# A two-layer attention block on one core: the opening's conditioning products, first transfers and first parts are laid out differently

## What is computed

```python
# layer 0
xn = x * rsqrt(mean(x*x) + 1e-6) * rms_w
scale, shift = split(cond @ w_cond)              # 512 x 512 weights
q, k, v = split((xn * (1 + scale) + shift) @ w_qkv)
q, k = rope(q), rope(k)
x = softmax(q k^T / 4) v @ w_out + x
# layer 1
xn = layer_norm(x, norm_w, norm_b)
q, k, v = xn @ q_w + q_b, xn @ k_w + k_b, (xn @ v_w + v_b) * mask
y = softmax(q k^T - 1e6 * (1 - mask)) v
scale, shift = split(silu(cond) @ emb_w + emb_b) # 512 x 512 weights
x = x + silu(layer_norm(y) * (1 + scale) + shift) @ out_w + out_b
```

## Time and profile before

| | |
|---|---|
| median of 3 runs | 514.0 us |
| the profiled execution | 513.65 us |
| its span, first to last instruction | 511.9 us |
| PE busy | 501.6 us (98%) |
| DVE, ACT, POOL busy | 80%, 68%, 43% |
| first row score starts | 40.31 us |
| mean granted clock of PE | 0.997 |

### The profile page before, as it was taken

One profiled execution on the slowest core, in us unless ns is written; L12 is line 12 of the kernel. 1 busy time (PEld: TensorE's weight loads), 2 busy tenths in 40 slices (PEclk: granted clock), 3 DMA queues, 4 the chain that ended last, 5 costly groups with the idle time before them and its releaser, 6 DMA issues.

```text
span 511.9 us, 9839 instructions
## 1 busy us (share of the span) xinstructions
PE 501.6 (98%) x3339; PEld 193.7 (38%) x3339; DVE 408.6 (80%) x1051; ACT 345.7 (68%) x679; POOL 219.9 (43%) x254
## 2 busy tenths in 40 slices
PE   9999899999999999999999999999999999999997
PEld 5553423333443244333443334332433333333234
DVE  4876897998897688966898678967899999999324
ACT  1552467776767675776768676777778778787863
POOL 3039749999143420832227430544573035005401
PEclk9999999999999999999999999999999999999999
DMA  6983232242214133110331123210431112211011
GB/s 243 351 273 101 75 103 75 66 143 82 77 53 125 41 125 121 46 43 8 119 125 44 42 90 114 68 33 32 125 124 44 43 43 85 81 46 44 2 41 42
DMA packets 43034, 45.26 MB, mean 88 GB/s; under 512 B 4436, under 2 KB 41572, under 8 KB 42600
## 3 DMA queue, kind: packets, MB, share of 16 engines
q1 hardware_dynamic: 42696, 42.79, 26.8%
q10 hardware_dynamic: 288, 1.84, 0.9%
HBM read 25.46 MB, written 18.87 MB: 87 GB/s over the span
## 4 chain that ended last, share of the span: by engine, by line
PE 74%; DVE 13%; issue 3%; ACT 2%; POOL 2%; DVEq 0%; ACTq 0%; POOLq 0%
PE bank L547 19%; PE bank L530 11%; PE bank L521 10%; PE bank L593 9%; PE bank L510 9%; DVE masked L870 8%; PE bank L621 5%; PE bank L604 5%; PE bank L562 2%; PE bank L582 2%; DVE row_max L873 1%; ACT probs L721 1%; PE bank L555 1%; PE bank L629 1%; POOL XN L844 1%
## 5 line engine op out<-in xcount | busy, mean ns | idle before, releaser
L721 ACT ACTIVATE probs<-bank 128x512 f32<-128x512 f32 x512 | 272.4, 601 | 82.0 <-PE bank L521 81.3
L873 DVE TENSOR_REDUCE row_max<-bank 128x1 f32<-128x512 f32 x256 | 163.0, 684 | 29.5 <-PE bank L530 27.8
L530 PE MATMUL bank<-k_s,q_s 64*128 64x512 f16 x512 | 183.0, 382 | 1.8 <-DVE row_max L873 1.2
L870 DVE CUSTOM_DVE_ANT_0 masked<-bank,mask_bias 128x512 bf16<-128x512 f32 x256 | 163.0, 687 | 13.0 <-PE bank L530 12.0
L510 PE MATMUL bank<-q_s,k_s 64*128 64x512 f16 x512 | 151.9, 381 | 0.9 <-ACT v_aug L789 0.5
L521 PE MATMUL bank<-shift,kx 64*128 64x512 f16 x512 | 148.8, 377 | 0.0
L547 PE MATMUL bank<-probs,v_aug 128*17 128x512 f32 x1024 | 135.4, 598 | 0.7 <-ACT probs L721 0.7
L530 PEld LDWEIGHTS bank<-k_s,q_s 64*128 64x128 f16 x512 | 46.3, 93 | 151.7 <-DVE row_max L870 67.1
L593 PE MATMUL bank<-xT,wqkv 128*128 128x512 f32 x128 | 61.8, 613 | 0.4 <-ACT xT L752 0.3
L521 PEld LDWEIGHTS bank<-shift,kx 64*128 64x128 f16 x512 | 46.9, 95 | 31.9
L510 PEld LDWEIGHTS bank<-q_s,k_s 64*128 64x128 f16 x512 | 31.7, 94 | 13.4 <-ACT probs L721 8.0
(11 more groups left out here) (112 smaller groups left out, 505.1 us busy)
## 6 DMA issues: line engine op xcount, KB each, us to landing
q_parts<-parts SPq DMA_DIRECT2D x64, 128.0 KB
k_parts<-parts SPq DMA_DIRECT2D x64, 128.0 KB
q_s<-q_parts SPq DMA_DIRECT2D x32, 256.0 KB, 2.8
k_s<-k_parts SPq DMA_DIRECT2D x32, 256.0 KB, 3.0
X<-in_x SPq DMA_DIRECT2D x4, 512.0 KB, 7.3
y<-X SPq DMA_DIRECT2D x7, 256.0 KB, 2.2
wc<-in_w_cond ACTq DMA_DIRECT2D x1, 1024.0 KB, 4.9
tables<-in_tables SPq DMA_DIRECT2D x4, 256.0 KB, 6.8
```

Source lines behind the costliest of these rows:

```text
L530: nc.tensor.matmul(bank, m.q_s[slot][rows, i, queries], m.k_s[slot][rows, i, :], start=True, stop=True).then_inc(q.d_made, 1)
L721: act.activation(m.probs[k][:, h, :], bank, ACT.Exp, scale=1.0 if s >= B * NG else float(DH) ** -0.5)\
L870: dve.tensor_tensor_reduce(m.masked[D["max", n, k, h] % ND][:, :], bank, m.mask_bias[:, b, :], 1.0, LOWEST, ALU.add, ALU.max, to)\
L873: dve.tensor_reduce(to, bank, AX.X, ALU.max).then_inc(q.d_done, 1)
```

## The change

- cond @ w_cond in two steps. Step 0: cond is stationary, padded to 32 columns, and w_cond moves, 4 matmuls of 512 columns, each block of 128 conditions in its own 32 output rows; ACT copies the 128x512 result to SBUF. Step 1: 4 matmuls with that copy as stationary operand and a matrix of zeros and ones, chosen, as moving one, which sum the four blocks and turn them round. silu(cond) @ emb_w is made in the same way, in two pieces instead of four.
- The first half of w_cond is loaded on ACT's queue, the second on SP's behind batch 0. The bulk is loaded in group 0 and emb_w behind the operands of group 2.
- POOL fills kx and makes chosen; DVE keeps kx0.
- DVE writes the second half of batch 0's xT, ACT the first.
- ACT normalises batch 2 behind ("qk", 0, 1, 3); POOL only batch 3, now behind the rotation of chunk 0 of batch 1.
- POOL issues the eight stores of the high parts and the two of chunk 2's low part; SP issues the six other low parts'. The high part of chunk 1 is made one step earlier in ACT's order.
- FIRST_BUSY goes from 14 to 17, the busy matmuls of the opening from 6, 6 and 3 to 4 and 2.

The diff, cut to its core (left out are names of semaphores and buffers, and waits that follow from the above; await_parts is what every wait for stored parts calls):

```diff
@@ -91,10 +91,11 @@
 PIECES = {
     0: ((), qk(0, 3, 1), (), ()),
     1: (qk(0, 3, 2), (), qk(0, 3, 3), ()),
-    2: ((("embed", 0),), (), (("embed", 1),), ()),
-    3: ((("embed", 2),), (), (("embed", 3),), ()),
+    2: ((), (), (), (("embed", 1),)),
     4: (v(0, 3)[:1], (), (), ()),
 }
+
+BESIDE_VALUES = {(1, 2): ("embed", 0)}
 for _b in range(B):
     _s = 5 + NG * _b
@@ -127,15 +128,16 @@
-FIRST_BUSY = 14
+FIRST_BUSY = 17
 LAST_BUSY = (10, 4)
 PIECES = spread(PIECES)
 OPENING = (
-    some(("modulate",)) + (("busy", 6),) + some(*turn("p0", 0)) + (("busy", 6),) + some(*qk(0, 0, 0, 1, 2, 3))
-    + some(*v(0, 0)[:1], *turn("p0", 1), *v(0, 0)[1:], *qk(0, 1, 0, 1, 2, 3), *v(0, 1), *turn("p0", 2)) + (("busy", 3),)
+    some(("modulate", 0)) + (("busy", 4),) + some(("modulate", 1), *turn("p0", 0)) + (("busy", 2),)
+    + some(*qk(0, 0, 0, 1, 2, 3))
+    + some(*v(0, 0)[:1], *turn("p0", 1), *v(0, 0)[1:], *qk(0, 1, 0, 1, 2, 3), *v(0, 1), *turn("p0", 2))
     + maxima(0, 0, 1, 0, 3) + some(*qk(0, 2, 0))
     + maxima(0, 0, 2) + maxima(0, 1, 1, 0) + some(*qk(0, 2, 1))
     + maxima(0, 1, 3, 2) + maxima(0, 2, 1) + some(*qk(0, 2, 2))
@@ -164,7 +166,7 @@
     PARTS_AT[8 + NG * _b] = ((B + _b, 0), (B + _b, 1))
     PARTS_AT[9 + NG * _b] = ((B + _b, 2), (B + _b, 3))
-HIGH_BEHIND = [("qk", 0, 0, 2), ("turn", "p0", 1, 0), ("turn", "p0", 1, 1), ("v", 0, 0, 1)]
+HIGH_BEHIND = [("qk", 0, 0, 2), ("qk", 0, 0, 3), ("turn", "p0", 1, 1), ("v", 0, 0, 1)]
 OUT_AT = {25: 0, 29: 1, 32: 2}
@@ -199,6 +201,8 @@
             yield op, s - 1
         if op == "maxima" and k == TURNED and exists(s + 1):
             yield op, s + 1
+        if op == "maxima" and (s, k) in BESIDE_VALUES:
+            yield "piece", BESIDE_VALUES[s, k]
         if op == "values" and (s or k):
             yield (op, s, k - 1) if k else (op, s - 1, KT - 1)
@@ -208,6 +212,12 @@
     for s in range(GROUPS):
         for k in range(KT):
             yield from key_tile(s, k)
+
+
+def for_dve(piece):
...
@@ -622,13 +655,24 @@
                                         start=(k == 0), stop=(k == CT - 1))
         last.then_inc(q.d_made, 1)
-    def conditioning(piece, vector, chunks):
-        bank = d_free(D[piece])
-        for c in chunks:
+    def conditioning(piece, vector):
+
+
+        kind, step = piece
+        if step == 0:
+            bank = a_free(A[piece])
             for k in range(KC):
-                last = nc.tensor.matmul(bank[:, c * B:(c + 1) * B], m.wc[:, k, c * P:(c + 1) * P], vector[:, k, :],
-                                        start=(k == 0), stop=(k == KC - 1))
-        last.then_inc(q.d_made, 1)
+                last = nc.tensor.matmul(bank[W32 * k:W32 * (k + 1), :], vector[:, k, :], m.wc[:, k, :],
+                                        start=True, stop=True, tile_position=(0, W32 * k), skip_group_check=True)
+            last.then_inc(q.a_made, 1)
+        else:
+            bank = d_free(D[piece])
+            pe.wait_ge(q.chosen_step, B)
+            pe.wait_ge(q.a_done, A[kind, 0] + 1)
+            for c in range(KC):
+                last = nc.tensor.matmul(bank[:, c * B:(c + 1) * B], m.conditions[:, c * P:(c + 1) * P], m.chosen[:, :],
+                                        start=True, stop=True)
+            last.then_inc(q.d_made, 1)
     def keep_busy(count, bank):
...
@@ -805,7 +858,20 @@
                 act.activation(last_tokens(m)[:, h, columns(p)], m.a_banks[CT * p + h][:, 0:2 * P], ACT.Silu,
                                bias=m.last_mod[:, 1, h, :], scale=m.last_mod[:, 0, h, :]).then_inc(q.last_silu, 1)
-    act.dma_start(m.wc[:, :, :], m.in_wc).then_inc(q.wc_in, 16)
+    def normal(b):
+        act.wait_ge(q.rstd0_made, b + 1)
+        if b == 2:
+            await_turned(act, q, ("p0", 0))
+        for t in range(TPB * b, TPB * b + TPB):
+            act.activation(m.XN[b % 2][:, t % TPB, :], m.X[:, t, :], ACT.Copy, scale=m.rstd["p0"][:, t:t + 1])\
+               .then_inc(q.xn_made, 1)
+
+    def high_part(i):
+
+        act.wait_ge(q.rope_dve, 3 * i + 3)
+        act.activation(m.parts[:, 0, i, :], m.roped[0][i % 2][:, :], ACT.Copy).then_inc(q.high_made, 1)
+
+    act.dma_start(m.wc[:, 0:KC // 2, :], m.in_wc[:, 0:KC // 2, :]).then_inc(q.wc_in, 16)
     act.wait_ge(q.cond_in, 16)
     act.activation(m.es[:, :, :], m.condT[:, :, :], ACT.Tanh, scale=0.5).then_inc(q.es_step, 1)
     act.wait_ge(q.x_in[0], 16)
@@ -822,20 +888,19 @@
         if op == "piece":
             piece, = at
             if piece == ("qk", 0, 0, 2):
-                act.wait_ge(q.rstd0_made, 2)
-                for t in range(TPB):
-                    act.activation(m.XN[1][:, t, :], m.X[:, TPB + t, :], ACT.Copy,
-                                   scale=m.rstd["p0"][:, TPB + t:TPB + t + 1]).then_inc(q.xn_made, 1)
+                normal(1)
             if piece[0] == "turn":
                 tokens(piece)
             if piece[0] == "qk":
                 queries_keys(piece)
             if piece[0] == "v":
                 token_values(piece)
+            if piece in (("modulate", 0), ("embed", 0)):
+                conditions(piece)
+            if piece == ("qk", 0, 1, 3):
+                normal(2)
             if piece in HIGH_BEHIND:
-                i = HIGH_BEHIND.index(piece)
-                act.wait_ge(q.rope_dve, 3 * i + 3)
-                act.activation(m.parts[:, 0, i, :], m.roped[0][i % 2][:, :], ACT.Copy).then_inc(q.high_made, 1)
+                high_part(HIGH_BEHIND.index(piece))
     last_batch()
...
@@ -931,18 +996,16 @@
     def opening():
         dve.memset(m.idle[:, :], 0.0).then_inc(q.idle_made, 1)
         dve.memset(m.ACC, 0.0).then_inc(q.acc_zero, 1)
-        for t in (m.kx0[:, :], m.kx[:, :, :]):
-            dve.memset(t, 0.0).then_inc(q.units_made, 1)
+        dve.memset(m.kx0[:, :], 0.0).then_inc(q.units_made, 1)
         token_statistics(0, 0, 1)
         dve.wait_ge(q.rstd0_made, 1)
         for t in range(TPB):
             normal_tile(dve, m, "p0", m.X[:, 0:TPB, :], m.XN[0], t, t).then_inc(q.xn0_made, 1)
         modulate()
         token_statistics(1, 1, 2)
-        dve.wait_ge(q.units_made, 2)
-        for t in (m.kx0[:, :], m.kx[:, :, :]):
-            for a in range(2):
-                dve.memset(t[ROWS * a:ROWS * a + 2], UNIT).then_inc(q.units_made, 1)
+        dve.wait_ge(q.units_made, 1)
+        for a in range(2):
+            dve.memset(m.kx0[ROWS * a:ROWS * a + 2], UNIT).then_inc(q.units_made, 1)
         dve.wait_ge(q.tables_in, 64)
         for i in range(4):
             rope_begin(i)
@@ -987,12 +1050,19 @@
            .then_inc(q.part_dve, 1)
     def modulate():
-        bank = made(D["modulate",])[:, 0:KC * B].rearrange("p (k b) -> p k b", b=B)
+        bank = made(D["modulate", 1])[:, 0:KC * B].rearrange("p (k b) -> p k b", b=B)
         dve.wait_ge(q.vecs_in, 16)
-        for h in range(CT):
-            dve.tensor_scalar(m.mod0_scale[:, h, :], bank[:, h, :], 1.0, m.vecs[:, RMS_W + h:RMS_W + h + 1],
-                              ALU.add, ALU.mult).then_inc(q.mod_made, 1)
-        dve.tensor_copy(m.mod0_shift[:, :, :], bank[:, CT:2 * CT, :]).then_inc(q.d_done, 1)
+        dve.tensor_copy(m.mod0_shift[:, :, :], bank[:, CT:2 * CT, :]).then_inc(q.mod_made, 1)
+        dve.tensor_scalar(m.mod0_scale[:, 0, :], bank[:, 0, :], 1.0, m.vecs[:, RMS_W:RMS_W + 1], ALU.add, ALU.mult)\
+           .then_inc(q.mod_made, 1)
+        dve.tensor_scalar(m.mod0_scale[:, 1, :], bank[:, 1, :], 1.0, m.vecs[:, RMS_W + 1:RMS_W + 2], ALU.add, ALU.mult)\
+           .then_inc(q.d_done, 1)
+
+        half_turned = made(D["turn", "p0", 0, 1])
+        dve.wait_ge(q.mod_made, CT)
+        dve.wait_ge(q.d_done, D["modulate", 1] + 1)
+        dve.tensor_scalar(m.xT[0][:, 1, :], half_turned, m.mod0_scale[:, 1, 0:1], m.mod0_shift[:, 1, 0:1],
+                          ALU.mult, ALU.add).then_inc(q.d_done, 1)
     def halve(piece):
@@ -1005,11 +1075,11 @@
         dve.tensor_scalar(m.halved[h], bank, m.mod1[:, 0, h, b:b + 1], m.mod1[:, 1, h, b:b + 1], ALU.mult, ALU.add)\
            .then_inc(q.d_done, 1)
-    def embed(piece):
-        c = piece[1]
-        bank = made(D[piece])
-        dve.tensor_scalar(m.e[:, c, :], bank[:, c * B:(c + 1) * B], 0.5, m.vecs[:, EMB_B + c:EMB_B + c + 1],
-                          ALU.mult, ALU.add).then_inc(q.d_done, 1)
+    def embed():
+        bank = made(D["embed", 1])[:, 0:KC * B].rearrange("p (k b) -> p k b", b=B)
+        dve.scalar_tensor_tensor(m.e[:, :, :], bank, 0.5,
+                                 m.vecs[:, EMB_B:EMB_B + KC].unsqueeze(2).broadcast_to([P, KC, B]),
+                                 ALU.mult, ALU.add).then_inc(q.d_done, 1)
     def last_batch():
...
@@ -1187,18 +1257,38 @@
                        pattern=[[-1, P]], channel_multiplier=1).then_inc(q.ident_made, 1)
     pool.wait_ge(q.ident_made, 3)
     pool.tensor_copy(m.ident16[:, :], m.ident[:, :]).then_inc(q.ident_made, 1)
+    pool.wait_ge(q.ident_made, 4)
```

(59 more changed lines are left out.)

81 lines of the change are left out of this document (55 added, 26 removed).

## The result

The changed kernel takes 511.19 us, the median of 5 runs (508.77 to 511.91), against 514.0 before: the ratio is 0.9937, 95% interval 0.992 to 0.9954. It is 2.8 us faster. I had forecast 507.0, 7.0 us faster, with a range from 505.0 to 510.5: the direction was right, the time lies outside the range. The profiled execution took 511.63 us (span 509.8), 2.0 us less than the one of before. Note the spread: 3.1 us between five runs, where the five of the kernel before beside them stay within 0.5. The fastest of the five, 508.77, lies inside the forecast's range; the trace is of another, slower one.

The account below looks back on a forecast made before the run. PE, busy 98% of the span, was taken to bound the kernel. The opening's 4.1 us plus the embedding product's 2.85 made 6.95 off the profiled 513.65, 506.7; with the median 0.35 above, forecast 507.0 us, range 505.0 to 510.5.

Parts of the forecast that it names:

- What bounds the kernel: Whole kernel: PE, busy 98% of the span; the opening's gain is set by PE's own chain and the operands' chain.
- Part 3: Operands' chain: rotation starts at 17.0, POOL's issues cost 1.0 us each, k_s issued at 33.0, row scores at 36.2.
- Part 4: Behind the opening: mask lands near 77.5, POOL about 0.6 us later than now; costed at nothing, 1.5 us without cover.
- Part 1: Up to the first projection: batch 0 lands at 6.05, XN at 10.55, projection starts at 12.55, 3.15 us earlier.
- Part 5: silu(cond) @ emb_w: four pieces, 3.85 us in all, become two of 0.5 us each, gaining 2.85 us.
- Part 2: PE's own chain: batch 2's turn no longer waits 0.93 us for XN; its projection starts at 36.9, 4.1 us earlier.
- Opening, sum: Opening up to batch 2's projection: both chains give 36.9 instead of 40.97, a gain of 4.1 us.
- sign that I had named for Part 4: An idle PE between 90 and 130 us would show the zero cost behind the opening wrong.
- The fourth: Rival behind the opening: the earlier start is given back at a later wait (mask, POOL's parts); 509 to 511, chance 0.06.
- The first: Rival: POOL's store issues cost over 1.3 us or land later; 508.5 to 512.5 at 0.18, nothing left at 0.03.
- second rivals: Rival: POOL's ten issues hold back batch 2; slower than before from 1.9 us each, 517 us at 2.2; chance 0.04.
- the third: Rival in the opening: clock stays at 1.2 GHz, batch 0 or tables land late; 0.5 to 1.1 us each, chance 0.14.

Follow-up runs that it names:

- x_first: Changed kernel with POOL's rotations held behind DVE's negations, and batch 0 of x loaded in halves on both queues ahead of w_cond: 509.29 us.
- one_step: Changed kernel with POOL's rotations held behind DVE's negations, and the opening's cond @ w_cond made in one step as before: 513.23 us.
- embed_four: Changed kernel with POOL's rotations held behind DVE's negations, and silu(cond) @ emb_w made in the old four pieces: 511.61 us.
- operands_first: Changed kernel with POOL's rotations held behind DVE's negations, and SP issuing operands of group s + 3 ahead of group s + 1's shift: 508.34 us.

## Why the prediction was wrong

Its steps, one by one.

**What bounds the kernel.** Right for the opening: in the trace of after PE works through from 13.57 to the end of batch 2's turn with no gap, and both chains meet there within 0.4 us, as Part 3 had it. Wrong for the rest; see Part 4.

**Part 1.** Batch 0 landed at 6.87, not 6.05: taking half of w_cond away from ahead of it gave 0.3 us of the 1.1. In x_first, where nothing is ahead, it landed at 4.23. XN came 0.8 us late (11.37, forecast 10.55), and that is most of the 1.0 by which 13.57 misses 12.55. The fills of kx cost nothing, as said, and the clock stayed at 2.4 GHz. That the product in two steps matters through the clock was only half seen; one_step puts it at 2.9 us.

**Part 1 and Part 5, the size of a float32 matmul.** This is the first mis-sized term. I took a row "x8" of the earlier trace rows for eight instructions of this kind. Each float32 matmul leaves two records, so four of them are the row: step 0 took 1.07 and step 1 1.03 (x8 each), where I had 0.5 and 0.5. The count that stands with the kernel before has it: 16 blocks are 32 records. The four old pieces were priced by rows and right, the two new ones at half, so 2.85 should have been about 1.8. Measured: 1.5 to 1.6 (embed_four, and groups 2 to 6 of operands_first).

**Part 2** held: the turn of batch 2 waits for nothing, and from it to ("qk", 0, 2, 0) it is 2.28 us.

**Part 3** held in its sum by luck, not in its terms. The rotation began at 17.98, because the chunk that it waits for came 1 us late with 13.57. An issue on POOL costs 0.53 us in eight of the ten and 0.66 in the first two, near the lower bound of 0.64 and far from the 1.0 taken; but POOL's last store ends at 30.45 and k_s is issued 3.4 us behind, not 1.93: SP waits 3.2 us for it to land. The errors nearly cancel: 33.0 forecast, 33.88 measured.

**Opening, sum:** 3.5 to 3.7 for 4.1. **Embedding:** 1.6 for 2.85. Together 5.3 for 6.95, and operands_first, where the table shows nothing given back, has 5.4 in its trace and 5.6 in its median. With these smaller terms alone the kernel would be at 508.3 to 508.7 us, inside the range of 505.0 to 510.5. What took it out of the range is the next step.

**Part 4 is the step that failed.** "I cost it at nothing" had two holes. I looked at whether POOL's products would be late for their readers; the low part of chunk 1 of batch 2 ended at 95.07 (forecast 93.7), and no wait of PE hangs on it. I did not ask what POOL's lateness does to DVE. The mask was issued at 73 and landed by 78.9 (forecast 77.5), POOL ran nearly without a pause from there to 130 us, and its operations fell on the negations of groups 3 and 6: 1.7 us by the table. And the operands' loads, which the earlier trace rows had shown to be tight, got later against a kernel that had got earlier: 1.4 us. The sum is 3.1 of the 3.4 us between the traces of after and operands_first; of the rest 0.05 is the opening's and most is what operands_first gains besides in groups 3 to 5. The sign that I had named for Part 4 was there, though faint: from 90 to 130 us PE is idle for 1.70 us in after and for 0.93 in the kernel before.

**The rivals.** The fourth, gain given back behind the opening, came true at 0.06; its 509 to 511 ends 0.2 short of the kernel's 511.2, since the terms too were too large. Its mechanism as told, a later wait that eats the earlier start, was right; which engine would wait for which it did not say. What I held against it was a misreading: a PE that is busy for 98% leaves no room for waits. The share is modelled from overlapping matmuls, its missing 2% are 10 us, and it was still 97% in after, with 3.1 us lost. In key tiles without a piece DVE sets the pace: its four maxima take 2.47 us, which is the pitch of such a tile on PE, and two operations of 0.17 us in front of them are on the path. The first and second rivals (dear issues on POOL) were wrong: 0.53 to 0.66 us. (At 1.4 us an issue the first one's own sum gives 509.5, not 509.) Of the third, batch 0 did land late and the clock did not fall.

Open: why some loads of k_s take 4 us and more (median of all 3.1). In after's trace the one that PE waited for longest has an instruction fetch in flight beside it, as this stretch from 150 to 154 us shows (its queues, and the load's time to landing):

```profile
q8 instruction: 1, 0.02, 1.5%
...
k_s<-k_parts SPq DMA_DIRECT2D x1, 256.0 KB, 4.3
```

The other loads do not bear this out as the cause: the one issued at 420.32 took 4.0 us with no fetch beside it and stores of y in flight, and the one at 311.80 had two fetches beside it and landed in 3.2. So the cause stays open. That an earlier issue removes the wait is shown: in operands_first some loads still take over 4 us, and PE waits for none.

## What to carry over

An earlier start is worth what the next meeting of engines lets through: price a moved piece also by what its engine's new phase does to short operations of others on the critical path, and look for loads with little lead. A wait that pins the long operations behind the short ones, and loads issued ahead of whatever the queue has to wait for, doubled the gain here (2.8 to 5.6 us). A busy share of 98% is no proof that nothing can be lost. A spread of 3 us in 5 runs of a kernel whose predecessor had 1.3 in 17 is a reason to look at more than one execution before a loss in one trace is taken for the loss of the median. And count a row's records against the code's instructions before using its mean as a price.

## What the runs showed of the hardware

- A DVE operation on 128x16 elements that reads SBUF can stand until the POOL operation under way ends: it ended 0.03 to 0.04 us behind it in the three cases read above, and took 0.68 to 1.19 us instead of 0.17. The Trainium skill, "SBUF — State Buffer", section "Who interferes with whom", says that a DVE instruction with two SBUF inputs contends with a GpSimd instruction that reads SBUF, and that whoever came first holds the shared pair for the whole instruction. By that rule, line 948, with two such inputs, waits, and the trace agrees: 1.17 and 1.19 us. The same section of the Trainium skill says that one with a single SBUF input waits only if it runs in a two-port mode; line 946 has one input and took 0.68 us here, and its like in the kernel before 0.86. No run shows which mode it ran in. I had used this very section for POOL's stores, and not for DVE's small operations.
- With cond moving in 4 columns the granted clock of one_step fell from 1.00 to 0.50 within 2 us of the start of the 32 matmuls and came back near 16.7, after 3 us of turns and matmuls on zeros. In the kernel before, with the same product, it fell over 3 us behind the start, in the stretch from 10 to 11 us (0.62), and was back at 1.00 from 14 us on.
- A store of 128 KB costs 0.53 to 0.66 us to issue on POOL, against 0.52 to 0.64 on SP, and takes 2.5 to 3.1 us to land (medians of the queries' and the keys' parts).
